# Softmax denominators summed on pixel partitions, image borders zeroed by ScalarE, and new orders on four engines with idle matrix products

## The reference, cut to what matters

```
x = x + block1(group_norm(x))
x = x + block2(group_norm(x))

block1(v):  a = v[:, :48];  xn = layer norm over the 48 channels
            q, k, v = bn(w_qkv @ xn)              # 16, 16 and 48 channels, 1024 pixels
            attn = softmax(q^T k / 4)             # 1024 x 1024 for each image
            out = v @ attn^T                      # 48 x 1024
            y = bn(w_proj @ relu(concat(out, v[:, 48:])))
block2(v):  channel attention (8 heads of 24 channels, 24 x 24 scores a head),
            a 1x1 and a 3x3 depthwise convolution of the values,
            t = 1x1 conv to 32 channels; 3x3 and dilated 7x7 depthwise convs of t (padding 1 and 9),
            a spatial gate (1x1 conv to 96, 3x3 depthwise, gelu product, 1x1 conv), a channel gate,
            (attended * sigmoid(spatial) + conv * sigmoid(channel)) @ w_pr + b
```

## Time and profile before

| | |
|---|---|
| median of 3 runs (range) | 431.94 us (430.26 to 434.22) |
| profiled execution | 430.68 us, span 428.9 us |
| PE busy | 356.4 us, 83% of the span |
| DVE busy | 287.5 us, 67% |
| ACT busy | 157.3 us, 37% |
| POOL busy | 35.7 us, 8% |
| mean granted TensorE clock | 0.926 |

### The profile page before, as it was taken

The page is one execution under the profiler, slowest core; times in us unless marked ns, Lnnn a source line. Parts: engine busy times, 40 slices in busy tenths (PEclk is TensorE's granted clock), DMA queues, the critical chain, the costliest instruction groups (busy, mean ns, idle before and its releaser), DMA issues. The chain is left out here.

```text
span 428.9 us, 4998 instructions
## 1 busy us (share of the span) xinstructions
PE 356.4 (83%) x1996; PEld 174.2 (41%) x1996; DVE 287.5 (67%) x490; ACT 157.3 (37%) x255; POOL 35.7 (8%) x45
## 2 busy tenths in 40 slices
PE   0649787989697898996978889887999887998996
PEld 0425443323255743331433454423345474444331
DVE  5637657447494589914542998678548878799464
ACT  1212252543602254472122731472262354443340
POOL 2102060002002100000101006000000001000000
PEclk9999998999997588899989996989999998798999
DMA  8530000000000012000002000030000003221004
GB/s 233 164 100 0 2 0 0 2 0 1 0 2 0 2 26 59 0 2 0 0 0 75 0 1 2 0 73 12 2 0 2 0 2 99 59 56 30 0 0 147
DMA packets 6067, 12.34 MB, mean 29 GB/s; under 512 B 2078, under 2 KB 2718, under 8 KB 5918
## 3 DMA queue, kind: packets, MB, share of 16 engines
q1 hardware_dynamic: 5532, 11.97, 10.5%
q10 hardware_dynamic: 514, 0.08, 0.1%
HBM read 5.32 MB, written 3.15 MB: 20 GB/s over the span
## 5 line engine op out<-in xcount | busy, mean ns | idle before, releaser
L1473 DVE SCALAR_TENSOR_TENSOR cx<-cpA,dw2w,cx 128x1024 f32<-128x1024 f32 x32 | 40.9, 1278 | 6.2 <-ACT cx L1946 6.1
L1484 DVE SCALAR_TENSOR_TENSOR dd<-spp,wt,dd 112x1024 f32<-112x1024 f32 x32 | 41.1, 1284 | 2.0 <-ACT dd L2032 1.1
L586 PE MATMUL psO<-pT,vt 128*64 128x512 f32 x96 | 29.6, 698 | 2.4 <-ACT pT L1916 2.2
L1473 DVE SCALAR_TENSOR_TENSOR cx<-cpB,dw2w,cx 128x512 f32<-128x512 f32 x32 | 23.9, 746 | 0.8 <-ACT cx L1946 0.8
L762 PE MATMUL psR<-up,wb 128*32 128x256 f32 (+1 forms) x336 | 23.5, 430 | 0.8 <-DMA up<-up 0.8
L2249 POOL TENSOR_TENSOR gr<-gvar,mhalf 128x2 f32<-128x2 f32 x8 | 6.0, 753 | 189.3 <-DVE gvar L1283 189.3
L1328 DVE TENSOR_REDUCE nm<-psB 128x1 f32<-128x1024 f32 x16 | 19.5, 1217 | 0.5 <-PE psB L556 0.4
L1340 DVE RECIPROCAL rb<-psA 112x512 f32<-112x512 f32 x3 | 10.1, 3355 | 13.0 <-PE psA L595 13.0
L1264 DVE BATCH_NORM_STATS2 st<-x 128x6 f32<-128x512 f32 x24 | 15.6, 685 | 3.6 <-DMA x<-x_dram 3.3
L1328 DVE TENSOR_REDUCE nm<-psA 128x1 f32<-128x1024 f32 x12 | 14.6, 1219 | 3.7 <-PE psA L556 3.7
L1916 ACT ACTIVATE pT<-psA 128x1024 f32<-128x1024 f32 x12 | 12.3, 1022 | 12.9 <-PE psA L576 12.9
(11 more groups left out here) (480 smaller groups left out, 768.4 us busy)
## 6 DMA issues: line engine op xcount, KB each, us to landing
up<-up SPq DMA_DIRECT2D x12, 200.0 KB, 3.1
x<-x_dram SPq DMA_DIRECT2D x4, 512.0 KB, 7.2
out_dram<-x SPq DMA_DIRECT2D x8, 256.0 KB, 2.1
wt<-params_dram SPq DMA_DIRECT2D x1, 1151.5 KB, 9.9
tp<-tp SPq DMA_DIRECT2D x8, 136.0 KB, 2.4
x<-x_dram SPq DMA_DIRECT2D x8, 128.0 KB, 5.7
out_dram<-x SPq DMA_DIRECT2D x8, 128.0 KB, 2.4
wt<-params_dram SPq DMA_DIRECT2D x1, 213.5 KB, 3.3
```

Of the source, the lines that this page charges most:

```text
L586: last = mm(s.o_ps[rows(n), :], s.vt[:, t, :], s.pT[t % 2][:, n * HB:(n + 1) * HB], start=(t == 0), stop=(t == NKT - 1))
L1473: v.scalar_tensor_tensor(acc, img, dw2w[:, blk, tap:tap + 1], acc, ALU.mult, ALU.add).then_inc(cv_s.of(c), 1)
L1484: v.scalar_tensor_tensor(acc, t.spp[:, dy:dy + HH, dx:dx + WW], par("w_spdw")[:, tap:tap + 1], acc, ALU.mult, ALU.add).then_inc(dv_s.of(c), 1)
```

## The change

- `denominators` transposes: four products with `osb` as the stationary operand give the sums of 128 pixels each on partitions, 2 columns a product, 8 columns in all. `inverse_denominators` inverts these 128x8 numbers. A new step `denominator_rows` on PE spreads them to rows with the same eight products as `rstd_rows`, and `attn_relu` multiplies by what stands in PSUM. A new semaphore phase carries that wait.
- `fill` on POOL is gone. `zero` on ACT writes the borders alone (and the three other tiles), 15 calls for each slot, by an activation with scale 0. `conv1_a` waits for those.
- The orders of PE, DVE, ACT, POOL and partly SP are new. PE's list now has 49 calls of `keep_warm`, a product of the identity with 256 columns of the weights into a part of PSUM that nobody reads. 19 of them stand ahead of the first `scores_t` of image 0, 10 between the last `pv` of image 1 and the first `score_rows` of image 2, 1 after the last `pv` of image 2, 12 from there to `proj1` of image 3, 5 in the rest, and 2 after the last product of the program.

```diff
@@ denominators
             def denominators(b):
-
                 s = one[SLOT1[b]]
                 pe.wait_ge(*oc_s(b, 1))
-                for n in range(2):
-                    last = mm(s.den_ps[rows(n), :], par("pick_den")[:, n:n + 1].broadcast_to([SPN + 1, SP2]),
-                              s.osb[0:SPN + 1, :], start=True, stop=True)
+                for t in range(4):
+                    last = mm(s.den_ps[:, 2 * t:2 * t + 2], s.osb[0:SPN + 1, t * P:(t + 1) * P], par("pick_den"),
+                              start=True, stop=True)
                 last.then_inc(dn_s.of(b), 1)
+
+            def denominator_rows(b):
+                s = one[SLOT1[b]]
+                pe.wait_ge(*dr_s(b, 1))
+                spread(s, s.row_ps).then_inc(db_s.of(b), 1)
...
-                v.reciprocal(s.rb[:], s.den_ps[0:SPN, :]).then_inc(dr_s.of(b), 1)
+                v.reciprocal(s.rT[:], s.den_ps[:, 0:NKT]).then_inc(dr_s.of(b), 1)
...
-                dve.wait_ge(*dr_s(b, 1))
+                dve.wait_ge(*db_s(b, 1))
...
-                    v.scalar_tensor_tensor(s.xm[0:PD, n, :], s.osb[p, :], 0.0, s.rb[p, :],
+                    v.scalar_tensor_tensor(s.xm[0:PD, n, :], s.osb[p, :], 0.0, s.row_ps[p, :],
...
+            def zero(i, k):
+
+                t = two[i]
+                tp = t.tp[:].rearrange("p (y x) -> p y x", x=PW)
+                up = t.up[:].rearrange("p (y x) -> p y x", x=UW)
+                e, far = PW - 1, UW - 9
+                o = (t.cpA[:, 0:PW:e, :], t.cpA[:, 1:e, 0:PW:e], t.cpB[:, 0:BH:BH - 1, :], t.cpB[:, 1:BH - 1, 0:PW:e],
+                     t.wmtB[:, P:2 * P], t.wmc[:], tp[:, 0:PW:e, :], tp[:, 1:e, 0:PW:e],
+                     up[:, 0:9, :], up[:, far:UW, :], up[:, 9:far, 0:9], up[:, 9:far, far:UW],
+                     t.spp[:, 0:PW:e, :], t.spp[:, 1:e, 0:PW:e], t.gmul[:])[k]
...
+                a(o, one_col.broadcast_to(list(o.shape)), ID, scale=0.0).then_inc(s_zero[i], 1)
...
-            def fill(i, k):
-
-                t = two[i]
-                pool.wait_ge(*nm_s(i, k + 1))
-                tile = (t.cpA, t.cpB, t.wmtB, t.wmc, t.tp, t.up, t.spp, t.gmul)[k]
-                g.memset(tile[:], 0.0).then_inc(s_fill, 1)
```

More of the change, by code:

```diff
@@ L291, in build @@
         s_gm = sem("group_matrices_spread")
+        s_zero = [sem(f"borders_zeroed_{i}") for i in range(2)]
         s_gav = sem("group_matrices_loaded")
@@ L513, in pixel_var, with spread @@
                 last.then_inc(var_s.of(b), 1)
+            def spread(s, ps):
+                for t in range(4):
+                    for n in range(2):
+                        last = mm(ps[rows(n), t * P:(t + 1) * P],
+                                  s.rT[:, 2 * t + n:2 * t + n + 1].broadcast_to([P, SP2]), ident,
+                                  start=True, stop=True)
+                return last
             def rstd_rows(b):
@@ L517, in rstd_rows @@
                 pe.wait_ge(*rT_s(b, 1))
-                for t in range(4):
-                    for n in range(2):
[L521 to L524, removed]
+                spread(s, s.row_ps).then_inc(rbp_s.of(b), 1)
             def qk_product(b, k):
@@ L903, in _ @@
             pv(0, 6)
+            score_rows(1, 6)
+            score_rows(1, 7)
+            pv(0, 7)
+            denominators(0)
             max_rows(1)
-            pv(0, 7)
+            denominator_rows(0)
             scores_t(1, 0)
@@ L908, in _ @@
             pv(1, 0)
+            proj1(0)
             scores_t(1, 2)
-            denominators(0)
             pv(1, 1)
@@ L924, in _ @@
             pv(1, 7)
+            keep_warm()
+            denominators(1)
+            denominator_rows(1)
             conv1_a(0)
+            proj1(1)
             conv1_b(0)
-            denominators(1)
             transpose_x(0, 0)
@@ L930, in _ @@
             transpose_x(0, 2)
-            proj1(1)
+            group_means(1, 1)
+            keep_warm()
+            keep_warm()
+            group_means(0, 2)
             gram_x(0)
             gram_w(0)
-            group_means(1, 1)
-            group_means(0, 2)
+            center(2)
             head_scores(0)
+            pixel_var(2)
             norms(0)
+            keep_warm()
+            keep_warm()
             k_norm_rows(0)
-            center(2)
-            pixel_var(2)
+            rstd_rows(2)
+            keep_warm()
+            keep_warm()
+            keep_warm()
+            keep_warm()
+            keep_warm()
             transpose_attn(0)
@@ L1552, in _ @@
             setup2_c()
+            layer_norm(1)
             setup2_d()
-            pixel_var(1)
-            channel_stats(0, 2, 2)
-            layer_norm(1)
-            setup2_e()
             q_low(1)
             k_low(1)
+            channel_stats(0, 2, 1)
+            channel_stats(0, 2, 2)
             v_copy(1)
```

592 lines of the change are left out of this document (325 added, 267 removed).

## The result

The changed kernel took 414.56 us (median of 4 runs, 411.62 to 417.34); the kernel before, run beside it, 432.06. The ratio is 0.9592, with a 95% interval of 0.9512 to 0.9672. Beside its parts on another chip it took 414.24 us against 435.3, ratio 0.9548 (0.9479 to 0.9617). The forecast was 412. The profiled execution took 414.26 us, its span 412.5 against 428.9. Executions of one kernel differ by some per cent, and those more than 1.5% above the fastest of their kernel are left out of the ratios.

What follows compares the result with a forecast made beforehand. The bound was PE's work (83% busy) plus its waits. Stage changes summed to -23.2 us, span 405.7; 4 of allowance made 409.7, then 1.8 and 1.3 up to the median made 412.8, taken as 412; range 401 to 427.

Steps and rivals of the forecast that it cites:

- Step 1: To the first scores_t of image 0, -7.5 us: layer_norm(0) -2.6, q/k/v products -1.9, row_max -0.8, setup2 and center -2.2.
- Denominators: From osb to the rows DVE reads, 4.5 us becomes 2.9; DVE regains 3.2 us an image, PE pays 1.3 as counted.
- Zeros: POOL's memsets go, giving DVE back some 2.4 and 2.7 us; ACT's 30 calls, 11 us in all, counted as nothing.
- The clock: Behind the first stage, idle products bring back the 28 us that low clock costs, all but 4.
- waits that I let stand: Stage 4 steps between small products +2.2 us, stage 5 sp_out_a +1.8, stage 6 branch of image 1 +5.1.
- the allowance: 4 of the 28 us of low clock cost left in, for low stretches that stay; span 405.7 becomes 409.7.
- the clock stays as it was: Rival: idle products do not lift the clock; 428 us, or 424 to 429 with some gaps filled; chance 0.2.
- the new lists pack tighter: Rival: without 5.1 us of branch gaps, 1.8 of sp_out_a and the allowance, 401 us; chance 0.12.
- Stage 6: To proj1 of image 3, +4.3 us: clock -7.4, wait -1.8, scalings -2.8; idle products +5.2, denominators +1.3, moved work 4.7, branch +5.1.
- Stage 7: To the end, -8.0 us: work moved out -4.7, low clock -5.4, five idle products +2.1.
- Stages 2 and 3: -2.0 us (setup2_e -4.4, clock -1.6, denominators +2.2, full PE +1.8), then -1.7 (denominators and reciprocal stop -2.8, exponentials +1.1).
- The orders: Each engine's new list followed stage by stage with the trace's durations; the stage changes sum to -23.2 us, span 405.7.

Runs made afterwards that it cites:

- gap_late: The changed kernel with five more idle products of 256 columns among transpose_attn(3) to transpose_attn(2); 412.9 us, ratio 0.9463 to the kernel before.

## Why the prediction was right, and where it wasn't

The total and the sign were right, and the sums and the memsets act as the prediction has them, with prices of their own. The account of the clock was wrong, and the total holds because two errors, of 27 and of 17 us, cancel for the most part; that it came within 1% is luck. Forecast and measured change of each stage, in us:

| stage | forecast | measured |
|---|---|---|
| 1, to `scores_t` of image 0 | -7.5 | -6.1 |
| 2, to `scores_t` of image 1 | -2.0 | -4.9 |
| 3, to its last `pv` | -1.7 | -2.9 |
| 4, to `score_rows` of image 2 | -3.5 | -3.2 |
| 5, to `proj1` of image 2 | -4.8 | -3.4 |
| 6, to `proj1` of image 3 | +4.3 | +8.3 |
| 7, to the end | -8.0 | -4.2 |
| sum | -23.2 | -16.4 |

**Step 1 held.** `layer_norm(0)` started at 25.32 us behind the statistic (25.5 said), and `score_rows` took 0.73 us. What is missing is a low stretch from 27.0 to 33.9 us, in which q, k and v products fall. That `scores_t` comes early does not rest on the idle products alone: the orders alone had it at 47.7 us.

**Denominators held.** PE's wait for `attn_relu` is gone, 8.1 us to 0.1, the reciprocal takes 0.21 us (0.16 said), and on the kernel before the new sums alone bring 9.3 us. I expected 9.9 us of waits less 5.2 of products there; the other 4.6 us come with 5 us less of recorded low clock, and with DVE being free 3.2 us an image sooner, and the two were not separated.

**Zeros: right that small DVE operations lose to POOL's memsets, wrong place and price.** I priced the copy of 9 columns (2.57 us before, 0.17 now) and the scalings before `k_norm_rows` (3.21 for two, 0.45 now). In the new order the memsets would have met `setup2_b`, with 5.4 us of DVE, 4.2 of PE and 17 us of low clock behind it: 12 us, not the 7.2 I took in stages 2 and 6. That ScalarE's calls cost nothing held as far as two kernels 1.8 us apart can show it.

**The clock: this step failed.** The prediction took back nearly all of 28 us and named 1.00 for 107 to 190 us and a mean near 0.98; the mean is 0.921 and recorded low clock 65 us as before. By my own test ("wrong if the clock's mean stays near 0.93") the reason is refuted, for all that lies behind the first stage. Priced as in the prediction, with each stage's own busy share, what is left in stages 4 to 7 costs 3.2, 3.3, 12.8 and 7.9 us, 27 in all, where I had left 4. Only in the first stage, whose gain I had read from a pair of products and not from the records, the clock did come back.

I had priced the idle products against the low clock of the old order. The new orders without them have 107 us of it (92 to 123 over ten runs) and a longer low start: the idle products do hold off low clock, 42 us in the records, and are worth 3.6% of the time (0.9912 against 0.9548), but most of that pays for what the orders brought.

**What cancelled it** are waits that I let stand. In stages 4 to 7 the forecast has PE's busy time fall by 10.3 us (26.2 of low clock, less 12.0 for 28 idle products and 3.9 for the sums) and its idle time by 1.7 (10.8 of waits gone, 9.1 new ones). Measured, the busy time rose by 16.3 us and the idle time fell by 18.8, from 43.3 to 24.5. The first is 27 us worse than forecast and the second 17 us better; the first three stages came out 2.7 us better, and the allowance was 4. Where the waits went can be read from the same stages of two other traces: PE idles 48.0 us in them with the orders alone, 34.3 in the kernel without idle products, and 24.5 with all. So the sums and the missing memsets go with 14 us less, and the idle products, which I had charged 12.0 us on top, stand for 10 us where PE would have waited.

The rival "the clock stays as it was" had the mean right and the time, 424 to 429, wrong by 10 us or more, because it too lets these waits stand. The rival "the new lists pack tighter" had that right, and its 401 was missed by the clock. What happened is both at once, which no rival priced.

**Stage 6** took -7.4 us for low clock going to zero. It went from 17.5 us of low clock to 27.6, that is from some 7.4 us of cost to some 13 (PE is 93% busy there), 13 us off. Against that stood +5.1 for waits in the branch of image 1: PE's idle time in the stage fell from 14.6 to 7.9 us, since idle products stand in some of these waits and PE no longer waits for `attn_relu`.

**Stage 7** took -5.4 us for the clock, which instead went from 12.6 us of low clock to 17: +2.5, so 8 off. Waits gave 5 of it back, idle PE 13.6 to 8.6 us. **Stages 2 and 3** gained 4.1 us more than said. I had put +1.8 us for PE being full and +1.1 for waits on exponentials; PE's idle time in them fell from 4.2 and 2.7 us to 1.2 and 0.9, and its busy time by 1.9 and 1.1.

**The orders** I counted stage by stage as a gain of their own. Alone they lose 3.5%. The whole change is worth what its parts are together: taking the sums, the idle products or the memset-free `setup2_b` away from the changed kernel costs 14, 17 and 12 us by the counted medians, while adding the sums to the kernel before brings 9, and adding the first 19 idle products 2, which is not told from nothing. Part of the 14 and the 12 is low clock that comes with the waits, so these parts don't add up.

## What to carry to other kernels

Where TensorE's clock moves, a wait can cost twice: the wait itself, and half of the low stretch that follows it (4.2 us and 17 us beside the memsets here). Price work that fills a gap at nothing until the gap is full. Price idle products against the low clock of the new order, not of the old one, and test each part by taking it away from the finished kernel as well as by adding it to the old one. Keep GpSimd's memsets away from the small VectorE steps that a chain waits for.

## What the runs showed of the hardware

- A recorded clock of 1.00 at the start of a trace is not a granted 1.00: without idle products `score_rows` takes 1.22 us at 35 us into the run, in a window of 52 us that says 1.00 throughout. The switch to the full clock stands where the record's first entry is, at 62.5 us in that trace:

```profile
58.69 1.22 PE L580 MATMUL psR<-qs,ks 98*128 98x512 f32 x2
63.01 0.70 PE L580 MATMUL psR<-qs,ks 98*128 98x512 f32 x2
```

  The first entry is at 10.0 us in the changed kernel, where the two records of an idle product go from 0.63 us each to 0.38, and at 51.4 us in the kernel before. From there on durations and clock agree. A mean clock can't be compared between kernels that differ in that part.
- The same list for PE up to 230 us gave a low start of 10 us in one trace and of 19 in another, and then its early low stretch at different times. For 38 to 58 us, the changed kernel and then gap_late:

```profile
38.00:58.00 20.00, 18.38 (x108) 10.11 (x106) 15.96 (x32) 8.31 (x9) 2.96 (x3) 1.00 0.00 1
```

```profile
38.00:58.00 20.00, 18.73 (x87) 10.39 (x88) 11.73 (x28) 5.93 (x7) 2.96 (x3) 0.66 0.00 1
```

  `proj1` of image 0 ended at 81.0 and at 84.5 us. Of a difference up to there, 3.5 us say nothing.
